# One read product per state over three channel groups in the selective scan of the last layer

## The reference, cut to what matters

```python
A = -jnp.exp(A_log)
A_bar = jnp.exp(dt_e * A)
Bu = dt_e * B_coef[:, :, None, :] * xc[..., None]

def step(hst, inp):
    Ab, bu, c = inp
    hst = Ab * hst + bu
    return (hst, jnp.einsum('bds,bs->bd', hst, c))
...
y = jnp.swapaxes(ys, 0, 1)
y = y + xc * D_skip
```

## Time and profile before

| | us |
|---|---|
| Median of three runs | 2568.31 |
| Lowest, highest | 2567.3, 2573.68 |
| The profiled execution | 2570.38 |
| Its span | 2567.1 |
| The scan function's four chunks, in the trace | 1505 to 1783 |

### The profile page before, as it was taken

One profiled execution on the slowest core, in us unless ns is written; L12 is line 12 of the kernel. 1 busy time (PEld: TensorE's weight loads), 2 busy tenths in 40 slices (PEclk: granted clock), 3 DMA queues, 4 the chain that ended last, 5 costly groups with the idle time before them and its releaser, 6 DMA issues. The chain is left out here.

```text
span 2567.1 us, 42132 instructions
## 1 busy us (share of the span) xinstructions
PE 2017.2 (79%) x13338; PEld 1496.5 (58%) x13338; DVE 1189.0 (46%) x2907; ACT 891.9 (35%) x1860; POOL 845.4 (33%) x759
## 2 busy tenths in 40 slices
PE   9745777987985885885985847777499957999998
PEld 8511223665764774664874312223489946999987
DVE  4348994233552112564112789998422234222222
ACT  1247783133342323343223645553222222122211
POOL 0204551013111444001454056664234412444443
PEclk9758997876986987896997879999699967999999
DMA  7000000000005663003773000000367725777774
GB/s 218 26 0 1 0 0 1 0 0 7 1 9 147 187 170 77 1 0 90 188 202 74 0 1 0 0 0 0 106 179 219 207 71 160 229 224 218 224 204 115
DMA packets 95935, 228.18 MB, mean 89 GB/s; under 512 B 22481, under 2 KB 60948, under 8 KB 87540
## 3 DMA queue, kind: packets, MB, share of 16 engines
q1 hardware_dynamic: 64564, 188.81, 23.1%
q0 software_dynamic: 31296, 38.48, 8.8%
HBM read 199.63 MB, written 27.62 MB: 89 GB/s over the span
## 5 line engine op out<-in xcount | busy, mean ns | idle before, releaser
L1962 PE MATMUL banks<-wt,hid 128*128 128x192 f32 x1932 | 347.5, 337 | 0.0
L1962 PEld LDWEIGHTS banks<-wt,hid 128*128 128x128 f32 x1932 | 328.3, 198 | 0.2
L1937 PE MATMUL banks<-xTblock,wt 128*128 128x256 f32 (+1 forms) x1464 | 267.7, 340 | 1.6 <-ACT xTblock L2020 1.2
L2160 DVE TENSOR_TENSOR hid<-sa,banks 128x512 f32<-128x512 f32 (+1 forms) x183 | 105.8, 578 | 339.2 <-ACT sa L2041 336.3
L2041 ACT ACTIVATE sa<-banks 128x512 f32<-128x512 f32 (+1 forms) x183 | 93.4, 510 | 481.5 <-PE banks L1948 476.6
L1937 PEld LDWEIGHTS banks<-xTblock,wt 128*128 128x128 f32 x1464 | 236.6, 193 | 23.7 <-issue 1.6
L1871 POOL DMA_INDIRECT sums<-yblock,put x96 | 152.8, 1592 | 287.9 <-DVE yblock L2175 177.9
L742 PE MATMUL banks<-g,consts 128*128 128x400 f32 x384 | 184.9, 572 | 60.5 <-DVE g L881 56.4
L1866 POOL DMA_INDIRECT xblock<-table,take x169 | 168.8, 999 | 183.6 <-DVE take L2134 114.2
L850 POOL TENSOR_TENSOR w<-u,spreadB 128x400 f32<-128x400 f32 x192 | 192.7, 1034 | 87.2 <-ACT spreadB L821 87.2
L875 DVE TENSOR_TENSOR_SCAN s<-banks,w 128x400 f32<-128x400 f32 x192 | 188.0, 979 | 4.2 <-POOL w L850 4.2
(11 more groups left out here) (379 smaller groups left out, 3446.4 us busy)
## 6 DMA issues: line engine op xcount, KB each, us to landing
wt<-L3f_packed SPq DMA_DIRECT2D x41, 1152.0 KB, 5.8
wt<-L_packed SPq DMA_DIRECT2D x60, 576.0 KB, 4.8
wt<-L3f_packed SPq DMA_DIRECT2D x41, 576.0 KB, 6.0
wt<-L3m_packed SPq DMA_DIRECT2D x20, 1152.0 KB, 5.8
wt<-L_packed SPq DMA_DIRECT2D x20, 675.0 KB, 5.1
wt<-L3m_packed SPq DMA_DIRECT2D x20, 577.0 KB, 5.8
pixels<-pixels SPq DMA_DIRECT2D x16, 375.0 KB, 5.1
wshift<-w_patch SPq DMA_DIRECT2D x8, 450.0 KB, 12.3
```

What stands on the lines that cost most here:

```text
L1937: nc.tensor.matmul(bank[:, n * j:n * (j + 1)], wt[:, v, cols(base, 2 * p + j)], xT[:, v, 0, 0:n], start=(j == 0), stop=False, skip_group_c ...
L1962: last = nc.tensor.matmul(bankY[s], hid[:, m, 128 * s:128 * (s + 1)], wt[:, v, DOWN_AT + DIM * m:DOWN_AT + DIM * (m + 1)], start=(m == 0 a ...
L2160: nc.vector.tensor_tensor(hid[:, 2 * p:2 * p + 2, 0:n], sa[:, (PAIRS * v + p) % 2, 0:2 * n].rearrange("p (m n) -> p m n", m=2), second[:, ...
```

## The change

`read` now covers the three groups of a state in one instruction of 1200 columns; `s` and `g_` are no longer four slots of 400 columns but two slots of 3 x 400. The row C is given to the product with a repeated dimension, so that each group meets the same 400 values. The recurrences stay one per job, their decays and the four `w2` slots as before. The read of state n-1 comes after the first recurrence of state n. PE's three sums of a state wait once, for the one product, and signal once. The branches for `bilinear=True`, which this call never took, are deleted.

```diff
+        w2 = t.sbuf("w2", [parts, SLOTS, CHUNK], st)
+        s, g_ = (t.sbuf(n, [parts, 2, groups, CHUNK], st) for n in ("s", "g"))
...
-                    def sum_states(j):
-                        n, g = divmod(j, groups)
-                        if j == 0:
+                    def sum_states(n):
+                        if n == 0:
                             pe.wait_ge(y_done, c + 1)
-                        pe.wait_ge(g_done, c * jobs + j + 1 + SLOTS)
-                        nc.tensor.matmul(acc[g][0:parts, 0:CHUNK], ident[0:parts, 0:parts], g_[:, j % SLOTS, :],
-                                         start=(n == 0), stop=(n == STATES - 1)).then_inc(summed, 1)
+                        pe.wait_ge(g_done, c * STATES + n + 3)
+                        for g in range(groups):
+                            last = nc.tensor.matmul(acc[g][0:parts, 0:CHUNK], ident[0:parts, 0:parts], g_[:, n % 2, g, :],
+                                                    start=(n == 0), stop=(n == STATES - 1))
+                        last.then_inc(summed, 1)
...
                     def recur(j):
-                        if bilinear:
-                            dve.wait_ge(w2_done, c * jobs + j + 1 + SLOTS)
-                        else:
-                            dve.wait_ge(bu_done, c * jobs + j + 2 + groups)
-                        dve.wait_ge(a_done, c * jobs + j + 1 + SLOTS)
-                        nc.vector.tensor_tensor_scan(s[:, j % SLOTS, :], decays[j % DECAYS],
+                        n, g = divmod(j, groups)
+                        dve.wait_ge(bu_done, c * jobs + j + 2 + groups)
+                        dve.wait_ge(a_done, c * jobs + j + 1)
+                        dve.wait_ge(g_done, c * STATES + n + 1)
+                        nc.vector.tensor_tensor_scan(s[:, n % 2, g, :], decays[j % DECAYS],
                                                      w2[:, j % SLOTS, :], 0.0, ALU.mult, ALU.add).then_inc(s_done, 1)
 
-                    def read(j):
-                        dve.wait_ge(s_done, c * jobs + j + 1 + SLOTS)
-                        dve.wait_ge(spread, c * STATES + j // groups + 1)
-                        nc.vector.tensor_tensor(g_[:, j % SLOTS, :], s[:, j % SLOTS, :],
-                                                bankC[(j // groups) % 2][0:parts, 0:CHUNK], ALU.mult).then_inc(g_done, 1)
+                    def read(n):
+                        dve.wait_ge(s_done, c * jobs + (n + 1) * groups + SLOTS)
+                        dve.wait_ge(spread, c * STATES + n + 1)
+                        dve.wait_ge(summed, c * STATES + n + 1)
+                        nc.vector.tensor_tensor(g_[:, n % 2], s[:, n % 2], bankC[n % 2][0:parts, 0:CHUNK].unsqueeze(1).to_broadcast([parts, groups, CHUNK]),
+                                                ALU.mult).then_inc(g_done, 1)
 
                     for j in range(jobs):
-                        dve.wait_ge(summed, c * jobs + j + 1)
...
-                        if not bilinear:
-                            recur(j)
-                        if j:
-                            read(j - 1)
...
-                    read(jobs - 1)
-                    dve.wait_ge(summed, c * jobs + jobs + SLOTS)
+                        recur(j)
+                        if j and j % groups == 0:
+                            read(j // groups - 1)
+                    read(STATES - 1)
+                    dve.wait_ge(summed, c * STATES + STATES + 2)
```

More of the change, by code:

```diff
@@ L677, in _, with scan @@
                     last.then_inc(y_done, 1)
-def scan(t, u, rate, coef, bc, direct, gain, y, bilinear):
+def scan(t, u, rate, coef, bc, direct, gain, y):
     nc = t.nc
@@ L712, in _ @@
                     nc.vector.tensor_copy(thirds[4 * STATES:6 * STATES, :], rest[:])
-        den_done, r_done, a_done, w1_done = t.sem("den_done"), t.sem("r_done"), t.sem("a_done"), t.sem("w1_done")
-        w2_done, s_done, g_done, summed = t.sem("w2_done"), t.sem("s_done"), t.sem("g_done"), t.sem("summed")
+        a_done, b_copied, bu_done, s_done, g_done, summed = (t.sem(n) for n in ("a_done", "b_copied", "bu_done", "s_done", "g_done", "summed"))
         b_spread, spread, y_done, a_zero = t.sem("b_spread"), t.sem("spread"), t.sem("y_done"), t.sem("a_zero")
-        w2, s, g_ = (t.sbuf(n, [parts, SLOTS, CHUNK], st) for n in ("w2", "s", "g"))
-        if bilinear:
-            den, r, w1 = (t.sbuf(n, [parts, SLOTS, CHUNK], st) for n in ("den", "r", "w1"))
-        else:
[L720 to L726, removed]
+        w2 = t.sbuf("w2", [parts, SLOTS, CHUNK], st)
+        s, g_ = (t.sbuf(n, [parts, 2, groups, CHUNK], st) for n in ("s", "g"))
+        spreadB = t.sbuf("spreadB", [parts, 2, CHUNK], st)
+        bankA, bankB, bankC, acc = (t.bank[1], t.bank[7]), t.bank[0], t.bank[2:4], t.bank[4:7]
         decays = [b[0:parts, 0:CHUNK] for b in bankA]
@@ L732, in _ @@
             def _(pe):
-                pe.sem_inc(summed, SLOTS)
+                pe.sem_inc(summed, 2)
                 with pe.Fori(0, CHUNKS) as c:
                     at = bass.ds(CHUNK * c, CHUNK)
-                    def sum_states(j):
-                        n, g = divmod(j, groups)
-                        if j == 0:
+                    def sum_states(n):
+                        if n == 0:
                             pe.wait_ge(y_done, c + 1)
-                        pe.wait_ge(g_done, c * jobs + j + 1 + SLOTS)
-                        nc.tensor.matmul(acc[g][0:parts, 0:CHUNK], ident[0:parts, 0:parts], g_[:, j % SLOTS, :],
-                                         start=(n == 0), stop=(n == STATES - 1)).then_inc(summed, 1)
+                        pe.wait_ge(g_done, c * STATES + n + 3)
[3 more added lines that the diff above has]
+                        last.then_inc(summed, 1)
                     def spread_row(bank, row):
@@ L749, in spread_b @@
                     def spread_b(n):
[L750 to L753, removed]
+                        pe.wait_ge(b_copied, c * STATES + n + 2)
                         pe.sem_inc(t.passed, 1)
-                        spread_row(bankB[n % len(bankB)], n).then_inc(b_spread, 1)
+                        spread_row(bankB, n).then_inc(b_spread, 1)
                     spread_b(0)
@@ L760, in _ @@
                             spread_b(n + 1)
-                        pe.wait_ge(g_done, c * jobs + (n - 1) * groups + SLOTS)
+                        pe.wait_ge(g_done, c * STATES + n + 1)
                         pe.sem_inc(t.passed, 1)
@@ L765, in _ @@
                         if n:
[L766 to L769, removed]
+                            sum_states(n - 1)
+                    sum_states(STATES - 1)
             @block.scalar
@@ L773, in _ @@
                 act.wait_ge(a_zero, 1)
-                for sem in (den_done, r_done, a_done):
-                    act.sem_inc(sem, SLOTS)
-                if not bilinear:
-                    act.sem_inc(b_copied, 2)
+                act.sem_inc(b_copied, 2)
                 nc.scalar.preload_act_table_set("natural_log_exp_and_others")
@@ L780, in _, with copy_b @@
                     at = bass.ds(CHUNK * c, CHUNK)
[L782 to L793, removed]
+                    def copy_b(n):
+                        act.wait_ge(b_spread, c * STATES + n + 1)
+                        act.wait_ge(bu_done, c * jobs + (n - 1) * groups + groups + 1)
+                        nc.scalar.activation(spreadB[:, n % 2, :], bankB[0:parts, 0:CHUNK], ACT.Identity).then_inc(b_copied, 1)
                     def decay(j):
@@ L797, in decay @@
                         act.wait_ge(s_done, c * jobs + j + 1 + SLOTS - DECAYS)
[L798 to L827, removed]
+                        act.sem_inc(t.passed, 1)
@@ new lines, in decay @@
+                        nc.scalar.activation(decays[j % DECAYS].rearrange("p (b t) -> p b t", t=SEQ)[:, :, 1:SEQ],
+                                             rate[:, g, at].rearrange("p (b t) -> p b t", t=SEQ)[:, :, 1:SEQ],
+                                             ACT.Exp, scale=coef[:, g, n:n + 1]).then_inc(a_done, 1)
+                    copy_b(0)
+                    for j in range(jobs):
+                        if (j + 1) % groups == 0 and j + 1 < jobs:
+                            copy_b((j + 1) // groups)
+                        decay(j)
@@ L829, in _ @@
             @block.gpsimd
             def _(pool):
[L831 to L851, removed]
@@ new lines, in _ @@
+                pool.sem_inc(bu_done, groups + 1)
+                with pool.Fori(0, CHUNKS) as c:
+                    at = bass.ds(CHUNK * c, CHUNK)
+                    for j in range(jobs):
+                        n, g = divmod(j, groups)
+                        pool.wait_ge(s_done, c * jobs + j + 1)
+                        pool.wait_ge(b_copied, c * STATES + n + 3)
+                        pool.sem_inc(t.passed, 1)
+                        nc.gpsimd.tensor_tensor(w2[:, j % SLOTS, :], u[:, g, at], spreadB[:, n % 2, :],
```

(38 more changed lines are left out.)

## The result

| | before | changed |
|---|---|---|
| Median of 20 runs each, us | 2568.39 | 2576.39 |
| Lowest, highest | 2558.7, 2574.49 | 2568.52, 2583.12 |
| Ratio to before, 95% interval | | 1.0031, 1.0021 to 1.0042 |
| The profiled execution, its span | 2570.38, 2567.1 | 2571.56, 2569.7 |
| From the first scan to the end of the last L898 (L829), in the trace | 275.36 | 284.27 |

What follows compares the result with a forecast made beforehand. The prediction took DVE to bound the changed function. Per chunk -1.9 + 1.6 + 0.3 + 1.0 = +1.0, so +4.0 us for four: 2572.3 us, counted as the same, range 2561 to 2584.

Steps and rivals of the forecast that it cites:

- The merging saves little: DVE's products: one of 1200 columns holds DVE 1.30 us against 1.39 for three, saving 0.09 us a state.
- rival 5: A removed product gives back all its fixed part, 0.25 us a state, no start stalls: 2558, faster; chance 0.06.
- 47 scans at 0.90 and 15 products at 1.30, -1.9 a chunk: DVE's work before a chunk's last scan starts: 61.8 us against 63.69, a gain of 1.9 us a chunk.
- a cover of 0.08: Third scan in a row: due at 1.80 us, its decay ready at 1.72; failing by as much again costs 6 us.
- My own sign of being wrong: DVE waiting for ACT in every state, scans 1.0 apart, or a granted clock below 0.9 over a chunk's middle.
- The new waits ask for work of two states ago: The added waits on `summed` and `g_done` concern work of two states ago; listed among what is covered.
- The chunk's end, +1.6: Three sums follow the last product: first L898 4.91 us behind the last scan's start against 3.28, +1.6 a chunk.
- The 1.95 from L898 to the next scan stay: Between chunks, the 1.95 us from the first L898 to the next chunk's first scan was to remain unchanged.
- The first four scans at POOL's pace, +0.3: At a chunk's start, four scans without a product between run 1.0 us apart, not 0.90: +0.3 us a chunk.
- The stall at the chunk's start, +1.0: Slow PE sums delay B's spread and job 8's decay to 11.1 against 10.1 wanted: +1.0 us a chunk, range 0 to 2.0.
- Rival 1: PE's longer idle in each state keeps the clock low, each state waits 1.1 us: 2638, slower; chance 0.05.
- Rival 2: DVE's scans in a row cost 1.0 us each, not 0.90: +12 us, 2584, slower; chance 0.10.

Runs made afterwards that it cites:

- kernel with three products: Changed kernel, each long product made as three of 400 columns, order and single signal kept; first scan to last L898's end 291.10 us against 284.27.
- reordered waits: Changed kernel, waits for POOL's product and ACT's decay placed last before each scan; first scan to last L898's end 279.22 us against 284.27.
- split of the last state: Changed kernel, each chunk's last state read in three separately signalled products; first scan to last L898's end 280.02 us against 284.27.
- early spread: Changed kernel, PE spreading B two states ahead and before a state's sums; first scan to last L898's end 280.78 us against 284.27.

## Why the prediction was right, and which term was off

The forecast was "the same, 4 us slower", with a range of 2561 to 2584; 8.0 us slower lies in it. But it is twice the 4 us, and just past the 7.7 that I had set as the least that counts as slower: the direction was right, and the size was not. Step by step:

- **The merging saves little.** Right. I said 0.09 us a state, from the overlap of 0.08 between neighbours. The long product is 1.38, as worked out, and holds DVE for 1.30. Against three products in a row it is worth 0.13 by the timeline. The kernel with three products was 6.83 us longer and not some 16, so rival 5 fell. (I had quoted the Trainium skill, VectorE: DVE Perf Modes, section The DRAIN you can't avoid, by half. The section also says that a next operation that is not held starts earlier, and in the traces here a next DVE instruction that waits for nobody starts 0.08 before the recorded end of the last one. The advice to minimize the number of operations stands in another section of that page, Rules for kernel authors.)
- **47 scans at 0.90 and 15 products at 1.30, -1.9 a chunk.** This step failed. An undisturbed scan behind a scan is 0.90, as I took it. But the third in a row came 0.98 behind the second, in 13 of the 16 states of a chunk. I had given the decay a cover of 0.08, with a lag of 0.03 from ACT to DVE, read from POOL's input ahead of a scan. The lag is 0.19 in the changed kernel and 0.10 with the waits reordered. So a state takes 4.09 and not 4.00, 1.1 a chunk and 4.3 us in all, and the whole gain of the merging went into a wait. My own sign of being wrong, DVE waiting for ACT in every state, came true, in pieces too short for the list of waits. In the text it stood as a bound ("if it fails by as much again, 6 us"), and it was the thing that happened. "The new waits ask for work of two states ago" was true and beside the point: the wait cost nothing by its semaphore, only by where it stood in the queue.
- **The chunk's end, +1.6.** Right: 4.91 foretold, 4.91 measured (4.89 in the other chunks), and the split of the last state took back 0.98 of it.
- **The 1.95 from L898 to the next scan stay.** Wrong by 0.19, three times; the reordered waits gave back 0.10 of it.
- **The first four scans at POOL's pace, +0.3.** Right: 0.99 apart.
- **The stall at the chunk's start, +1.0.** Right in its mechanism, slow sums with the spread of B behind them. It measured 3.5 us over the four chunks, not 4, in the waits and again in the early spread's kernel.
- **Rival 1, the lower clock stays.** It did not: the window of 1515 to 1560 has 1.00.
- **Rival 2, scans in a row cost 1.0.** Half true, for one of the two pairs (0.98), and for a reason other than DVE's pace. The prediction named that reason beside it: decays that come late.

In the first chunk that is: a first to last scan of 63.90 for 63.69 before, where 63.1 was foretold; an end of 4.91 for 3.28; a next scan after 2.14 for 1.95. The other chunks lose more, 64.20 for 63.67 from first to last scan, since their wait at the start is longer. Over all four chunks the scans and products cost 1.8 us where I had foretold a gain of 2.4, the ends 6.5 where I had 6.4, and the next scans 0.6 where I had nothing: 8.9 and not 4.0.

Three slips in the prediction's sums change nothing of this. A chunk has 32 pairs of neighbouring scans without a product between them, not 31. By its own terms (4.8 due, less 0.06, 0.12, 0.49 and 0.63) the sums and the spread become the bound at 3.5 us, not 3.6. And the range is said to take in rival 5, but that rival's own 2558 lies below the range's 2561.

## What to carry to other kernels

In this kernel merging instructions on the busiest engine was worth only 0.09 to 0.13 us for each two removed, so first count what the merged one makes wait: everyone who could start behind its first part now starts behind its last, and at a loop's end that is not covered. Where an alternation of long and short work is broken up, look at the producer whose time the short work had covered. And of several waits ahead of an instruction write the one that comes last nearest to it, and those that are long fulfilled first.

## What was new about the hardware

The place of a late wait in DVE's queue moved a start by 0.09 us: 0.19 behind ACT's end with a register instruction between the late wait and the scan, 0.10 without it. Behind POOL the same two kernels gave 0.22 and 0.12, and the kernel before, where the scan itself held the wait, 0.03, so these lags are DVE's own. How soon behind ACT a scan starts that holds ACT's wait itself, no kernel here shows. And products of one kind in a row lasted longer: the first 0.55, the second and third 0.56 each (three in 1.51 or 1.50), each still starting 0.08 before the end of the one ahead.
